# Layer norms of an attention stage in groups of four tiles, moments by aggregation, and half of the queries normalised one stage earlier

## The reference, cut to what matters

```python
x = x + delta_rule_attention(_layernorm(x))     # 16 heads, a scan over the 512 tokens
q = _layernorm(x)                               # (x - m) / sqrt(v + 1e-5)
logits = where(mask == 0, -9e15, q @ ctx.T / 16)
a = softmax(logits) @ ctx
x = x + _layernorm(a) * gamma + beta            # "attended"
h = _layernorm(_layernorm(x)) * g + b           # "hidden"
# both linear layers: ternary weights, inputs rounded to int8 by the 0.995 quantile of |input|
x = x + qlinear(gelu(qlinear(h, w1)), w2)
```

## Time and profile before

| what | value |
|---|---|
| time of 3 runs | 1075.34, 1076.52 (median), 1081.33 us |
| profiled execution | 1070.09 us |
| its span | 1068.2 us |
| TensorE matmuls busy | 905.3 us, 85% |
| VectorE busy | 912.0 us, 85% |
| ScalarE busy | 655.0 us, 61% |
| GpSimd busy | 480.2 us, 45% |

### The profile page before, as it was taken

One profiled execution on the slowest core, in us unless ns is written; L12 is line 12 of the kernel. 1 busy time (PEld: TensorE's weight loads), 2 busy tenths in 40 slices (PEclk: granted clock), 3 DMA queues, 4 the chain that ended last, 5 costly groups with the idle time before them and its releaser, 6 DMA issues.

```text
span 1068.2 us, 19463 instructions
## 1 busy us (share of the span) xinstructions
PE 905.3 (85%) x6084; PEld 690.0 (65%) x6091; DVE 912.0 (85%) x2684; ACT 655.0 (61%) x1597; POOL 480.2 (45%) x667
## 2 busy tenths in 40 slices
PE   7799999999999999999999998899898601795066
PEld 6586877877787787787777876666666400342044
DVE  5789999988999999999999999765777898799887
ACT  3666776766667666666666664556587341795085
POOL 5444355345446536535535534314486660780000
PEclk9799999999999999999999999999999955798579
DMA  9700000000000000003000000213300000000012
GB/s 164 129 6 6 6 10 8 6 6 11 6 6 10 8 6 9 8 6 127 9 6 8 10 6 8 89 63 120 118 2 0 1 0 0 1 1 1 1 62 96
DMA packets 28573, 30.49 MB, mean 29 GB/s; under 512 B 5548, under 2 KB 23864, under 8 KB 28472
## 3 DMA queue, kind: packets, MB, share of 16 engines
q1 hardware_dynamic: 28256, 29.12, 10.8%
q10 hardware_dynamic: 216, 0.14, 0.0%
HBM read 20.85 MB, written 4.19 MB: 23 GB/s over the span
## 4 chain that ended last, share of the span: by engine, by line
PE 71%; DVE 20%; issue 5%; POOL 2%; ACT 2%; DVEq 0%; ACTq 0%; POOLq 0%
PE ps L1887 8%; PE ps L1879 7%; PE psG L1841 6%; PE psY L1855 5%; PE ps L1818 5%; PE psX L1855 4%; PE psX L1933 3%; PE psY L1933 3%; PE ps L1999 3%; PE psG L1835 3%; PE ps L1947 2%; PE psX L2020 2%; PE ps L2187 2%; PE psG L1836 2%; PE psY L2020 1%
## 5 line engine op out<-in xcount | busy, mean ns | idle before, releaser
L529 POOL TENSOR_TENSOR arena<-arena 128x256 f32<-128x256 f32 x32 | 23.4, 730 | 305.8 <-DVE arena L1160 299.9
L634 ACT ACTIVATE arena<-ps 128x512 f32<-128x512 f32 x128 | 73.0, 596 | 40.1 <-PE ps L1879 39.6
L1879 PE MATMUL ps<-work 32*128 32x256 f32 x512 | 93.7, 406 | 2.5 <-ACT work L680 1.8
L497 POOL TENSOR_SCALAR_AFFINE_SELECT arena<-arena 128x2048 f32<-128x2048 f32 x32 | 92.1, 2879 | 2.2
L599 ACT ACTIVATE arena<-ps,nparity 32x256 f32<-32x256 f32 x124 | 51.2, 459 | 47.4 <-PE ps L1818 47.0
L1879 PEld LDWEIGHTS ps<-work 32*128 32x128 f32 x512 | 62.2, 186 | 19.7 <-issue 12.0
L1841 PE MATMUL psG<-arena 128*128 128x512 f32 x128 | 72.9, 655 | 1.1 <-DVE arena L1226 1.1
L1171 DVE TENSOR_TENSOR arena<-arena 128x256 f32<-128x256 f32 (+1 forms) x96 | 66.6, 694 | 3.4
L1174 DVE TENSOR_REDUCE arena<-arena 128x64 f32<-128x256 f32 (+1 forms) x96 | 65.9, 686 | 3.3
L1855 PEld LDWEIGHTS psY<-work,arena 128*128 128x128 f32 x512 | 60.0, 195 | 12.8 <-DVE arena L1243 11.6
L1818 PE MATMUL ps<-work,arena 128*128 128x64 f32 x496 | 60.6, 276 | 7.8 <-DVE work L1186 7.8
(11 more groups left out here) (349 smaller groups left out, 2612.2 us busy)
## 6 DMA issues: line engine op xcount, KB each, us to landing
arena<-in_mask_BxSxS_ik SPq DMA_DIRECT2D x8, 1024.0 KB, 6.5
xs<-arena SPq DMA_DIRECT2D x256, 16.0 KB, 1.8
arena<-in_ctx SPq DMA_DIRECT2D x8, 512.0 KB, 4.2
out<-xs SPq DMA_DIRECT2D x32, 128.0 KB, 1.7
arena<-in_x SPq DMA_DIRECT2D x8, 288.0 KB, 18.0
arena<-in_L_ffn_w SPq DMA_DIRECT2D x2, 1024.0 KB, 22.6
arena<-in_x SPq DMA_DIRECT2D x16, 96.0 KB, 6.3
arena<-in_L_attn_w_qkvb SPq DMA_DIRECT2D x2, 512.0 KB, 4.9
```

Of the source, the lines that this page charges most:

```text
L497: G.affine_select(out=pairs, in_=pairs, compare_op=ALU.is_ge, fill=0.0, base=0, pattern=[[0, NH], [-CT, B], [0, CT]], channel_multiplier=1 ...
L634: A.activation(attn[j % 2][:, r * 512:(r + 1) * 512], ps[(2, 0)[r % 2]][:, :], ACT.Copy).then_inc(att_out, 1)
L1879: last = M.matmul(ps[(2, 0)[r % 2]][:, f * 2 * P:(f + 1) * 2 * P], kq[j % 4][rows, f * P:(f + 1) * P], qe[rows, f].rearrange("p e t -> p ( ...
```

## The change

The norms go in nine groups of consecutive tiles, seven of four and two of two. The six operations of `moments` are replaced by bn_aggr, one for each tile (`aggregated`), which writes a tile's mean and variance side by side. The roots stay on VectorE in ten small operations a block (`roots`, with the same `rsqrt`), in the step after the aggregation. All hidden tiles but the last eight are normalised by step 31.

The query rows of the first two quarters (`EARLY`, 16 tiles) are normalised in the scan (`early_query`, in the chunks of `QUERIES_AT`) and kept in the place of the later output y, from which TensorE turns them. Their roots, and those of the third quarter, are made on GpSimd in three operations (`row_norms`, one of them a power of -0.5); those of the last quarter by GpSimd in four (`last_roots`) after VectorE's eight aggregations. GpSimd adds beta to the early tiles in one go at the start of the stage.

```diff
@@ -57,33 +57,39 @@
 PIECES = [0, 2] + [4 * b - 4 for b in range(2, B + 1)]
 LAST = [max(n for n in range(NT) if ORDER[n][0] == b) for b in range(B)]
 
-GROUPS = [(0, 2), (2, 4), (4, 6), (6, 7), (7, 8)]
+EARLY = [n for n in range(NT) if ORDER[n][1] < 2]
+LATE = [n for n in range(NT) if ORDER[n][1] >= 2]
+BETA_ORDER = EARLY + LATE
+QUERIES_AT = {20: 2, 21: 2, 22: 2, 23: 2, 27: 1, 28: 1, 29: 2, 30: 4}
+ROW_NORMS_AT = {18: 0, 26: 1, 30: 2}
+
+GROUPS = [(4 * q, 4 * q + 4) for q in range(7)] + [(28, 30), (30, 32)]
 ON_POOL = 28
-GROUP_OF = [[b0 <= b < b1 for b0, b1 in GROUPS].index(True) for b, _ in ORDER]
-LAST_OF = [max(n for n in range(NT) if GROUP_OF[n] == q) for q in range(len(GROUPS))]
...
-NORMED_AT = by_step([n + 1 + split for n, split in zip(LAST_OF, SPLIT_ATTENDED)])
-XNORM_AT = [max(s for s in NORMED_AT if GROUP_OF[NORMED_AT[s][-1]] == q) + 2 for q in range(len(GROUPS))]
-SPLIT_HIDDEN = [n < NT - 2 for n in XNORM_AT]
-HIDDEN_AT = {n: [2 * (n - 16), 2 * (n - 16) + 1] for n in range(16, 20)}
-HIDDEN_AT.update({n: [2 * (n - 20), 2 * (n - 20) + 1] for n in range(24, 28)})
-ABS_AT = {n + 2: tiles for n, tiles in HIDDEN_AT.items()}
-LARGEST_AT = {n + 3: tiles for n, tiles in HIDDEN_AT.items()}
-HIDDEN_AT.update({31: range(16, 24), 33: range(24, 28), 36: range(28, 32)})
-ABS_AT.update({34: range(16, 24), 37: range(24, 28), 38: range(28, 32)})
-LARGEST_AT.update({36: range(16, 20), 38: range(20, 32)})
+GROUP_OF = [[first <= n < end for first, end in GROUPS].index(True) for n in range(NT)]
+
+
+def in_pairs(first):
+
+    return {first[q] + k: [4 * q + 2 * k, 4 * q + 2 * k + 1] for q in range(len(first)) for k in range(2)}
+
+
+NORMED_AT = in_pairs([4 * q + 5 for q in range(7)])
+NORMED_AT.update({31: [28, 29], 33: [30, 31]})
+RESIDUAL_AT = {n + 2: tiles for n, tiles in NORMED_AT.items() if n < 31}
+RESIDUAL_AT.update({33: [28, 29], 35: [30, 31]})
+HIDDEN_AT = in_pairs([4 * q + 11 for q in range(5)] + [30])
+HIDDEN_AT.update({34: [24, 25, 26, 27], 35: [28, 29], 37: [30, 31]})
+ABS_AT = in_pairs([4 * q + 13 for q in range(5)] + [32])
+ABS_AT.update({35: [24, 25], 36: [26, 27], 37: [28, 29], 38: [30, 31]})
+LARGEST_AT = in_pairs([4 * q + 13 for q in range(5)] + [33])
+LARGEST_AT.update({36: [24, 25], 38: [26, 27, 28, 29, 30, 31]})
+SCALED_AT = {n: tiles for n, tiles in HIDDEN_AT.items() if n < 34}
+SCALED_AT.update({34: [24, 25], 36: [26, 27]})
+LAST_AT = {36: [28, 29], 38: [30, 31]}
+ATTENDED_KNOWN = {GROUPS[q][1] - 1: q for q in range(9)}
+HIDDEN_KNOWN = {**{4 * q + 8: q for q in range(7)}, 33: 7, 35: 8}
+ATTENDED_ROOTS = {**{4 * q + 4: q for q in range(7)}, 30: 7, 32: 8}
+HIDDEN_ROOTS = {**{4 * q + 9: q for q in range(7)}, 35: 7, 36: 8}
 STEPS = 39
...
@@ -520,6 +529,15 @@
                 t = wraw_piece(p)
                 G.tensor_scalar(t, t, ROUND + 1.0, ROUND - 1.0, ALU.min, ALU.max).then_inc(bounded, 1)
 
+            def row_norms(w):
+
+                cols = slice(w * B, (w + 1) * B)
+                pool.wait_ge(squares_known, (w + 1) * B)
+                own(G.tensor_scalar(qr[:, cols], s2[:, cols], 1.0 / D, LN_EPS, ALU.mult, ALU.add))
+                own(G.tensor_tensor(qr[:, cols], qr[:, cols], half, ALU.pow))
+                G.tensor_tensor(qs[:, cols], qs[:, cols], qr[:, cols], ALU.mult).then_inc(q_known, 1)
+
...
@@ -530,6 +548,8 @@
                 mask_attention(j)
                 if j + 3 < NCK:
                     key_norms(j + 3)
+                if j in ROW_NORMS_AT:
+                    row_norms(ROW_NORMS_AT[j])
                 if 12 <= j < 16:
...
@@ -538,7 +558,10 @@
 
                 b, w = ORDER[n]
                 i = w * B + b
-                pool.wait_ge(q_ready, n + 1)
+                if n in EARLY:
+                    pool.wait_ge(q_early, len(EARLY))
+                else:
+                    pool.wait_ge(q_ready, LATE.index(n) + 1)
                 G.tensor_tensor(xs[:, i, :], xs[:, i, :], xb_s, ALU.add).then_inc(xbeta_ready, 1)
 
...
@@ -561,17 +584,32 @@
                 G.tensor_tensor(t, t, fb_s, ALU.add).then_inc(h_ready, 1)
 
             pool.wait_ge(const_in, 64)
-            for n in range(3):
+
+            def roots(first, end, root, gain, floor, shift, ready):
+
+                own(G.tensor_scalar(root[:, first:end], s2[:, first:end], gain, floor, ALU.mult, ALU.add))
+                own(G.tensor_tensor(root[:, first:end], root[:, first:end], half[:, 0:end - first], ALU.pow))
+                own(G.tensor_scalar(s1[:, first:end], s1[:, first:end], -1.0, None, ALU.mult))
+                G.tensor_tensor(shift[:, first:end], s1[:, first:end], root[:, first:end], ALU.mult).then_inc(ready, 1)
+
+            def last_roots():
+
+                pool.wait_ge(last_moments, 1)
+                roots(3 * B, NT, qr, 1.0, LN_EPS, qs, last_known)
...
+            for n in EARLY[0:10]:
+                beta_added(n)
+            last_roots()
+            for n in EARLY[10:] + [n for n in LATE if n < 3]:
                 beta_added(n)
             for n in range(STEPS):
-                if n + 3 < NT:
+                if n + 3 in LATE:
                     beta_added(n + 3)
                 for k in NORMED_AT.get(n, ()):
                     if k < ON_POOL:
                         attended_added(k)
-                for k in HIDDEN_AT.get(n, ()):
-                    if k < ON_POOL:
-                        hidden_scaled(k)
+                for k in SCALED_AT.get(n, ()):
+                    hidden_scaled(k)
 
...
@@ -817,11 +855,23 @@
 
                 b, w = ORDER[n]
                 i = w * B + b
-                act.wait_ge(q_known, 2 if w == 3 else 1)
-                if n >= 2:
-                    act.wait_ge(q_T, n - 1)
-                A.activation(xn[n % 2][:, :], xs[:, i, :], ACT.Identity, bias=qs[:, i:i + 1],
+                if n in EARLY:
+                    return
+                k = LATE.index(n)
+                if w == 3:
+                    act.wait_ge(last_known, 1)
+                else:
+                    act.wait_ge(q_known, 3)
+                if k >= 2:
+                    act.wait_ge(q_T, LATE[k - 2] + 1)
+                A.activation(xn[k % 2][:, :], xs[:, i, :], ACT.Identity, bias=qs[:, i:i + 1],
                              scale=qr[:, i:i + 1]).then_inc(q_ready, 1)
+
+            def early_query(i):
+
+                act.wait_ge(q_known, i // B + 1)
+                A.activation(y[:, i, :], xs[:, i, :], ACT.Identity, bias=qs[:, i:i + 1],
+                             scale=qr[:, i:i + 1]).then_inc(q_early, 1)
 
...
@@ -926,6 +977,8 @@
                 if exists(j):
                     early_work(j)
                     early_stats(j)
+                    for _ in range(QUERIES_AT.get(j, 0)):
+                        early_query(next(early_tiles))
...
@@ -1278,25 +1331,29 @@
                 v.wait_ge(xb_ready, j + 1)
                 V.tensor_tensor(xc[:, j, :], xc[:, j, :], ps[2][:, 0:D], ALU.add).then_inc(x_done, 1)
 
-            def early_norms():
-
-                v.wait_ge(squares_known, 3 * B)
-                n = 3 * B
-                own(V.tensor_scalar(T[0][:, 0:n], s2[:, 0:n], 1.0 / D, LN_EPS, ALU.mult, ALU.add))
-                rsqrt(qr[:, 0:n], T[0][:, 0:n], T[3][:, 0:n])
-                V.tensor_tensor(qs[:, 0:n], qs[:, 0:n], qr[:, 0:n], ALU.mult).then_inc(q_known, 1)
-
-            def moments(cols, gain, floor):
-
-                a, b, c, e = (cols(stats[:, :, k]) for k in (1, 4, 2, 5))
-                total, apart, var = (cols(T[k]) for k in range(3))
-                own(V.tensor_tensor(total, a, b, ALU.add))
-                own(V.tensor_tensor(apart, a, b, ALU.subtract))
-                own(V.tensor_tensor(apart, apart, apart, ALU.mult))
-                own(V.tensor_tensor(var, c, e, ALU.add))
-                own(V.scalar_tensor_tensor(var, apart, 0.25 * D, var, ALU.mult, ALU.add))
-                own(V.tensor_scalar(var, var, gain / D, floor, ALU.mult, ALU.add))
-                return total, var
+            def aggregated(first, end, known):
+
+                for n in range(first, end):
+                    last = V.bn_aggr(sums_of[:, 2:4, n], stats[:, n, :])
+                last.then_inc(known, 1)
+
+            def roots(first, end, root, gain, floor, ready):
+
+                var = T[2][:, first:end]
+                own(V.tensor_scalar(var, s2[:, first:end], gain, floor, ALU.mult, ALU.add))
+                rsqrt(root[:, first:end], var, T[3][:, first:end])
+                V.scalar_tensor_tensor(shift1[:, first:end], s1[:, first:end], -1.0, root[:, first:end],
+                                       ALU.mult, ALU.mult).then_inc(ready, 1)
+
+            def attended_roots(q):
+
+                v.wait_ge(att_moments, q + 1)
+                roots(*GROUPS[q], rstd, 1.0, LN_EPS, yn_known)
+
+            def hidden_roots(q):
+
+                v.wait_ge(hid_moments, q + 1)
+                roots(*GROUPS[q], scale1, 1.0 + LN_EPS, LN_EPS * LN_EPS, hn_known)
 
             def last_stats():
...
```

(46 more changed lines are left out.)

55 lines of the change are left out of this document (15 added, 40 removed).

## The result

| | before | after |
|---|---|---|
| median of the runs of this comparison | 1077.13 us (1075.34 to 1081.33, 7 runs) | 1070.67 us (1065.98 to 1072.69, 7 runs) |
| profiled execution, its span | 1070.09, 1068.2 us | 1065.98, 1064.1 us |
| TensorE, VectorE busy | 905.3, 912.0 us | 911.3, 916.4 us |
| ScalarE, GpSimd busy | 655.0, 480.2 us | 655.6, 488.3 us |

The ratio of after to before is 0.9926, with a 95% interval of 0.9901 to 0.9951. The forecast was 1070.1 us, 0.9941 of its 1076.5. VectorE does 4.4 us more work and the kernel is faster all the same: the total of the engine says nothing here, as the prediction argued.

A forecast was written before the change was run, and what follows sets the result against it. The attention stage was taken as bound by TensorE's 4.70 us steps plus late VectorE minima, then by VectorE's own work. Ring +2.8 and tail -9.2 gave -6.4 us, from 1076.5 to 1070.1; range 1062 to 1081.

The forecast's parts named there:

- the scan: Stage before the attention stage's first logits: early queries and moved small operations cost 0, bounded at 1 us.
- the ring: Attention stage, logits of step 0 to those of step 27: late minima on VectorE make it 2.8 us slower.
- the tail: From step 27's logits to the first quantile sample: VectorE's own work sets it, 53.5 after 62.7 us, gain 9.2.
- The price of the aggregation: One bn_aggr on VectorE: taken as 0.11 us, never blocked by GpSimd, 0.04 and 0.46 kept as bounds.
- The rule that spoke against the change: Fixed term of about 150 cycles per VectorE instruction: four aggregations would cost 0.65 us and not 0.45.
- A cycle of four: Four attention steps, two with ten roots each on VectorE: loses 1.8 us, 1.5 in the first and 0.3 next.
- The blocked operation: Small VectorE operation held up by GpSimd's additions: 0.54 us against 0.20 free, so 0.34 more.
- the three sources: Tail's 9.2 us gain: 16 tiles' hidden work done earlier, eight fewer maxima, only 19 of 70 small operations meeting GpSimd.
- the roots never meet GpSimd: Rival on blocking in the ring: ring gains 2.4 us, with half the tail's blocking gone 1061 us; chance 0.20.
- always: Rival: roots meet GpSimd as often as it is busy, 53 of 80 operations blocked, 1084 us; chance 0.13.
- the aggregation costs 0.46: Rival on bn_aggr's price: 8 us before late minima and 4 in the tail, 1082 us; chance 0.09.
- the tail's gain is not had: Rival: ScalarE or GpSimd delivers late and VectorE waits, leaving only the ring's 2.8 us loss, 1079 us; chance 0.08.

The follow-up runs named there:

- before_aggr: The kernel before with only bn_aggr per tile replacing five of the six operations of moments, groups, queries and roots kept: ratio to before 0.9902.
- aggr_twice: The changed kernel with each of the 72 aggregations made twice, the first into a place nothing reads: ratio to before 0.9961.
- pool_roots: The changed kernel with all 18 blocks of roots on GpSimd, four operations each: ratio to before 0.9822.
- four_left: The changed kernel with hidden norms of tiles 16 to 19 put off to step 31, their maxima to step 36: ratio to before 0.9934.
- queries_late: The changed kernel with no early queries, all 32 tiles normalised to queries in the attention stage: ratio to before 0.9973.
- six_moments: The changed kernel with five small VectorE operations on a whole group in place of one aggregation per tile: ratio to before 1.0115.

## Why the prediction was right, step by step

**The total.** 1070.1 against 1070.67 us. On the profiled execution it was 1063.7 against 1065.98: the scan gave +3.5 that the sum did not hold, the ring +0.2 and the tail -1.3 against their forecasts. With equal scans the change is worth 7.5 us by the traces, where the forecast was 6.4. The medians differ by 6.5, which is nearer to the forecast than the stages are.

**The price of the aggregation.** Taken as 0.11, with bounds of 0.04 and 0.46, measured 0.074 in the queue; before_aggr moves the time in the amount of this price, and so do the steps of aggr_twice. The rule that spoke against the change (the Trainium skill, page "VectorE: DVE Perf Modes", the section on the TRN2 errata) gave an estimated 0.16 each. That fits the duration of one, 0.159, by this trace, but not what it costs in a row of four, and aggr_twice shows that the latter counts. The other one (the Trainium skill, page "SBUF — State Buffer", the section on the two separate sides) would spare the aggregation from blocking, and the trace agrees: none of the 72 was stretched, where ones of the same size that stand beside them were.

**The ring.** A cycle of four was to lose 1.8 us, 1.5 and 0.3; it loses 2.1 (20.88 less 18.8), 1.3 and 0.7. Step 16 is as forecast to 0.3 us: three blocked operations of ten. In step 17 the hidden roots were to be free and two of them were blocked, 2.74 us in place of 2.0: the first pair of GpSimd's additions ends only at 783.54, and the second pair begins at 785.05, inside the block. The first eight steps cost nothing more than before (37.98 us for 38.21), as said for the start of the stage. That the difference of the rings came out to 0.2 us is luck in part. Against the undisturbed ring of pool_roots, 127.18, the kernel before loses 5.6 us and not the 4.6 counted, and the changed one 8.6 and not 7.4 (four cycles of 1.8 and 0.2); the two errors nearly cancel.

**The blocked operation.** The mean of the earlier trace rows, 0.54 us, mixes blocked and free ones. A blocked one holds the queue mostly 0.60 to 0.70 us and a free one 0.20, so the surcharge is 0.44 and not 0.34. The tail hid this mistake, by luck: 15 operations were blocked there and not 19, and 15 x 0.44 is about 19 x 0.34. What sets the price of a blocked one is where in an addition it begins, as it ends with the addition.

**The tail.** 53.5 forecast, 52.2 measured, by the walk on VectorE: 70 small operations as counted, 15 of them blocked. Of the three sources named, the small operations are the main one: with the aggregation alone 5.1 of the 10.5 us are had, four_left gives 2.0 to four of the earlier hidden tiles, and the rest belongs to the smaller groups and the order together, which was not taken apart further.

**The scan.** No cost of the 16 early queries was forecast and queries_late showed none. What they bring was overlooked: the prediction counted them in the scan alone, and the 2.5 us that they save in the ring (4.2 with the clock) are in no term. The sum came out near without it, since the walk had fewer blocked operations in the second step of a cycle (none) than even the kernel with early queries has (two). The power on GpSimd took 1.65 us for eight columns, over the 1.08 of the dearest small operation of the earlier trace rows, and was hidden as the text said.

**The rivals.** That the roots never meet GpSimd, or always, was decided by the counts of 3 and 2 of 10 in a cycle. That the aggregation costs 0.46, or that the tail's gain is not had, is excluded by the rows.

**What the prediction did not see** is how the gain is made up. The aggregation alone gives 8.7 us; groups of four, with 18 blocks of roots for 10, together with the early queries and the hidden order, give 5.4 more in the tail and take 6.7 in the ring. Without the early queries they would take another 2.5, or 4.2 with the clock. Where the roots lie decides: on GpSimd the same groups are worth 21.6 us.

## What to carry to other kernels

Small operations that run beside GpSimd have two prices a factor of three apart, and they count in full where a late instruction of the pacing chain stands behind them; count them there, and not in the engine's total. A change that is a bundle should be priced and tried part by part: here one of its parts gives all of the gain, and another has to pay back what a third costs. Before a late stretch is put down to a change, compare the granted clock of the stretch and cut the times at marks; the stages then repeated to 0.1 us while the whole varied by 8. That they repeat does not make them free of the clock: in a variant whose steps keep TensorE waiting, read the granted clock step by step before you call its loss the price of the edit. In six_moments more than half of the ring's loss was the clock's.

## What the runs showed of the hardware that was not expected

- The scan's end moved between 691.9 and 701.1 us over the executions, with the granted clock of a few stretches (1.00, 0.93 or 0.86 from 85 to 110 us): 692 at 1.00, 695.5 to 696.9 at 0.93, 699.7 to 701.1 at 0.86. What decides the clock in an execution stays open, and the kernel seems to bear on it: the five executions with the scan of the kernel before showed 1.00 twice and 0.86 three times, the nine of the others 0.93 seven times and 0.86 twice. On average it made no difference: the first logits came at 696.9 in the five and at 697.2 in the nine.
- The granted clock also fell inside the ring in five traces, where TensorE's work of a step then took 6.28 us for 4.58.
- A small operation of VectorE that begins inside one of GpSimd's additions waits for its end: all 38 long ones of the changed kernel end 0.02 to 0.03 us behind an addition.
- GpSimd's power costs by the column of each row: 0.73 us for 2, 1.04 for 4 and 1.65 for 8, where its other small operations take 0.2.
- bn_aggr lasts 0.159 us and costs 0.074 in a row of them, and is not stretched beside GpSimd's additions, while small operations of the same width are, from 0.16 to 0.57 to 0.65 us.
